# Four engine programs of a fused transformer kernel, up to the main loop, written out in another order

## The reference

```python
x = x + tanh(g_xattn[0]) * L0_xattn(layernorm(x), ctx)   # softmax(query key^T) of the context mixes x
x = x + tanh(g_ffn[0])   * L0_ffn(layernorm(x))          # 8-bit activations, ternary weights, 704 wide
x = x + tanh(g_xattn[1]) * L1_xattn(layernorm(x), ctx)   # 16 heads of 128, rmsnorm on q and k, Wo
x = x + tanh(g_ffn[1])   * L1_ffn(layernorm(x))          # 64 experts, top 8, and a shared expert

def bit_linear(x, w, g):      # used twice in L0_ffn, with silu(gate) * up between
    xn = rms_norm(x, g)
    scale = 127 / clip(max|xn|, 1e-5);  xq = clip(round(xn * scale), -128, 127) / scale
    return xq @ weight_quant(w).T
```

## Time and profile before

| | |
|---|---|
| median of 3 runs | 615.78 us (615.51 to 616.06) |
| the profiled execution, its own time | 616.09 us |
| its span | 614.3 us |
| TensorE busy | 603.3 us (98%) |
| VectorE busy | 477.9 us (78%) |
| ScalarE busy | 422.7 us (69%) |
| GpSimd busy | 236.7 us (39%) |
| granted TensorE clock | 1.00 of full speed, all through |

### The profile page before, as it was taken

One profiled execution on the slowest core, in us unless ns is written; L12 is line 12 of the kernel. 1 busy time (PEld: TensorE's weight loads), 2 busy tenths in 40 slices (PEclk: granted clock), 3 DMA queues, 4 the chain that ended last, 5 costly groups with the idle time before them and its releaser, 6 DMA issues.

```text
span 614.3 us, 11619 instructions
## 1 busy us (share of the span) xinstructions
PE 603.3 (98%) x3644; PEld 522.6 (85%) x3644; DVE 477.9 (78%) x1139; ACT 422.7 (69%) x1082; POOL 236.7 (39%) x282
## 2 busy tenths in 40 slices
PE   8979999999999999999999999999999999999997
PEld 6757899999999999999998888888887888887886
DVE  3999988987777787688876787788777676777776
ACT  6999999888888888889897344465444444443442
POOL 5999998576665566656662020000000000000000
PEclk9999999999999999999999999999999999999999
DMA  8513202000000000000030545453856466545640
GB/s 299 196 53 102 95 11 78 2 2 2 2 2 2 1 2 2 1 2 1 11 121 3 170 147 154 129 171 96 216 156 167 116 176 175 156 154 149 195 128 34
DMA packets 33653, 56.47 MB, mean 92 GB/s; under 512 B 12800, under 2 KB 13504, under 8 KB 33600
## 3 DMA queue, kind: packets, MB, share of 16 engines
q1 hardware_dynamic: 33312, 55.82, 30.4%
q10 hardware_dynamic: 288, 0.00, 0.0%
HBM read 53.45 MB, written 1.31 MB: 89 GB/s over the span
## 4 chain that ended last, share of the span: by engine, by line
PE 89%; DVE 5%; ACT 4%; issue 1%; POOL 1%; DVEq 0%; ACTq 0%; POOLq 0%
PE bank L310 25%; PE bank L312 25%; PE bank L311 25%; PE bank L985 4%; PE bank L960 2%; PE bank L952 2%; DVE hs L2088 1%; PE bank L912 1%; PE bank L1026 1%; PE bank L829 1%; DVE attT_lo L2182 1%; PE bank L835 1%; ACT att L1575 1%; ACT w L1478 1%; PE bank L815 1%
## 5 line engine op out<-in xcount | busy, mean ns | idle before, releaser
L1623 ACT ACTIVATE inter_hi<-inter 128x512 fp32r<-128x512 f32 x63 | 39.8, 632 | 140.5 <-DVE inter L2287 140.5
L310 PE MATMUL bank<-xnT_hi,front_hi 128*128 128x512 f32 (+1 forms) x260 | 102.0, 392 | 0.0
L312 PE MATMUL bank<-xnT_hi,front_lo 128*128 128x512 f32 (+1 forms) x260 | 101.7, 391 | 0.0
L311 PE MATMUL bank<-xnT_lo,front_hi 128*128 128x512 f32 (+1 forms) x260 | 101.6, 391 | 0.0
L2291 DVE TENSOR_TENSOR inter_lo<-inter,inter_hi 128x512 fp32r<-128x512 f32 x63 | 43.6, 692 | 37.9 <-ACT inter_hi L1623 37.3
L1575 ACT ACTIVATE att<-bank,shift,rq 128x256 f32<-128x256 f32 x128 | 71.3, 572 | 0.0
L596 POOL TENSOR_TENSOR att<-att,rowinv 128x512 f32<-128x512 f32 x60 | 63.1, 1067 | 11.1 <-DVE rowinv L2187 11.1
L2260 DVE TENSOR_TENSOR prod<-gate_s,bank 128x512 f32<-128x512 f32 x63 | 43.3, 687 | 21.6 <-PE bank L312 19.5
L2170 DVE TENSOR_REDUCE rowmax<-bank 128x2 f32<-128x512 f32 x64 | 43.6, 686 | 20.7 <-PE bank L312 20.4
L311 PEld LDWEIGHTS bank<-xnT_lo,front_hi 128*128 128x128 f32 x260 | 48.9, 188 | 11.3
L312 PEld LDWEIGHTS bank<-xnT_hi,front_lo 128*128 128x128 f32 x260 | 48.8, 188 | 11.3
(11 more groups left out here) (273 smaller groups left out, 1811.7 us busy)
## 6 DMA issues: line engine op xcount, KB each, us to landing
w_all<-w_rows SPq DMA_DIRECT2D x128, 128.0 KB, 3.0
raw<-in_expert_w SPq DMA_DIRECT2D x32, 384.0 KB, 3.5
wvo_raw<-in_expert_w SPq DMA_DIRECT2D x16, 384.0 KB, 3.5
e_more<-in_expert_w SPq DMA_DIRECT2D x16, 384.0 KB, 3.6
raw<-in_head_qk SPq DMA_DIRECT2D x8, 384.0 KB, 3.1
wvo_raw<-in_head_vo SPq DMA_DIRECT2D x4, 384.0 KB, 3.8
w_keep<-in_head_vo SPq DMA_DIRECT2D x4, 384.0 KB, 3.3
gate_raw<-in_gate_wT SPq DMA_DIRECT2D x2, 704.0 KB, 9.0
```

The source lines that it names most:

```text
L310: pe.matmul(out, l_hi, r_hi_, start=start, stop=False, skip_group_check=True)
L311: pe.matmul(out, l_hi, r_lo_, start=False, stop=False, skip_group_check=True)
L312: return pe.matmul(out, l_lo, r_hi_, start=False, stop=stop, skip_group_check=True)
L1623: act.activation(inter_hi[:, slot, :], inter[:, slot, :], ACT.Copy).then_inc(a_Ihi, 1)
```

## The change

No call is added or removed, but for waits: the calls of the four lists stand in another order, and TensorE's list has more `wait_ge` lines, most of them for values that a later wait of the same place implies. GpSimd gets a wait for `v_Klo` ahead of `root_3(1)`, and ScalarE one for `v_tg` ahead of `high_m(1, 7)`. SyncE's transfers, the loop and all that follows are as before.

```diff
TensorE
+            turn_att(2, 4)
             sum_abs([0, 1], 0)
-            turn_att(2, 4)
+            turn_rows_0(2, 7)
+            pe.wait_ge(t_abs, 1)
             pe.wait_ge(v_abs, 1)
             mix(1, 0)
-            sum_abs([2], 5)
-            turn_rows_0(2, 7)
-            fuse_vo(0, 6)
+            mix(2, 4)
+            pe.wait_ge(t_oA, 2)
             pe.wait_ge(v_xA, 2)
             keep_busy(0, 8)
             turn_q1(0, 0)
-            pe.wait_ge(a_x0, 3)
-            turn_q1(1, 7)
+            sum_abs([2], 5)
+            fuse_vo(0, 6)
+            pe.wait_ge(t_abs, 2)
+            pe.wait_ge(v_abs, 3)
+            proj_k(0, 5, True)
             gate_0(0)
             up_0(0)
-            mix(2, 4)
+            turn_q1(1, 7)
             gate_0(1)
...
+            gate_0(6)
+            pe.wait_ge(t_y2, 1)
+            pe.wait_ge(v_xB, 1)
+            fuse_vo(3, 6)
             turn_q1(7, 5)
-            gate_0(6)
-            pe.wait_ge(v_xB, 2)
+            pe.wait_ge(t_M, 3)
+            pe.wait_ge(a_Mhi, 3)
+            turn_q2(2, 4)
             up_0(6)
-            fuse_vo(3, 6)
             gate_0(7)
+            down(2, 5)
             up_0(7)
-            turn_q2(2, 4)
ScalarE
             abs_down()
-            split_w(0)
             turn_gate(0)
-            exp_A(3, 3)
-            copy_att(2, 4)
+            load_table(ACT.Silu)
             turn_gate(1)
-            copy_rows_0(2, 7)
             copy_q1(0, 0)
-            load_table(ACT.Silu)
+            high_ctx()
             silu_0(0)
VectorE
+            max_A(0, 2)
             stats_0(0)
             aggr_0(0)
             stats_0(1)
-            max_A(0, 2)
             max_A(1, 6)
...
             absmax_2(4)
-            round_2(2)
-            times_up_0(6)
             low_m(1, 7)
-            round_2(3)
-            absmax_2(5)
-            low_w(2)
             times_up_0(7)
             low_rows(0, 0, 1)
+            low_k(0, 0)
+            absmax_2(5)
GpSimd
             round_gate(1)
             power_1(0)
             root_1(1)
+            scale_back_1(0)
+            power_0(3)
+            scale_gain(g2, l_g2)
+            normalise_0(6)
+            limit_1(0)
+            normalise_0(7)
             power_1(1)
```

More of the change, by code:

```diff
@@ L1128, in _ @@
             gate_0(4)
-            fuse_vo(1, 7)
+            proj_k(1, 6, True)
+            up_0(4)
+            pe.wait_ge(t_y1, 5)
             pe.wait_ge(a_s1, 5)
@@ L1175, in _ @@
             turn_k(1, 0)
+            turn_q2(4, 2)
+            pe.wait_ge(t_y2, 4)
+            pe.wait_ge(v_xB, 4)
+            turn_q(1, 3)
             turn_q2(5, 6)
-            pe.wait_ge(a_q2, 5)
-            down(4, 2)
-            turn_q(1, 3)
             pe.wait_ge(a_sqQ, 8)
             proj_k(3, 4, True)
+            down(4, 2)
+            pe.wait_ge(t_q2, 6)
             pe.wait_ge(a_q2, 6)
             turn_q2(6, 6)
-            fuse_vo(6, 5)
+            scores(0)
+            pe.wait_ge(t_K, 4)
@@ L1196, in _ @@
+            scores(1)
+            proj_k(4, 3, True)
             proj_q(3, 4, True)
-            down(7, 7)
-            pe.wait_ge(v_Qlo, 2)
-            proj_k(4, 3, True)
-            pe.wait_ge(a_exp, 4)
-            scores(1)
+            pe.wait_ge(a_sqQ, 12)
+            turn(0, 0)
+            pe.wait_ge(t_K, 5)
+            pe.wait_ge(a_rawK, 5)
+            turn(0, 1)
+            pe.wait_ge(v_Klo, 3)
+            fuse_vo(7, 6)
+            proj_q(4, 5, True)
             pe.wait_ge(v_xB, 8)
@@ L1263, in _ @@
             output(2, 1)
[L1264 removed]
+            turn(4, 0)
             values(3)
[L1266 removed]
             scores(5)
[L1268 removed]
+            pe.wait_ge(v_Qlo, 7)
+            proj_q(8, 7, True)
             pe.wait_ge(a_sqQ, 32)
@@ L1722, in _ @@
             copy_q2(1, 4)
-            square_h(4)
+            act.wait_ge(v_tg, 8)
             high_m(1, 7)
             copy_q1(6, 5)
+            square_h(4)
+            split_w(2)
+            whole_m(2, 4)
             square_h(5)
-            whole_m(2, 4)
+            silu_0(6)
             copy_q1(7, 5)
-            silu_0(6)
-            split_w(2)
+            copy_q2(2, 4)
             split_w(3)
@@ L2338, in _ @@
             round_1(0)
-            inv_A(3)
+            norm_A(3)
             round_1(1)
-            norm_A(3)
+            weight_scale(1, 5, INTER * HID)
+            add_A(2, 4)
             absmax_1(1)
-            low_w(0)
+            stats_1(2)
+            inv_scale(1)
             inv_max_1(1)
+            aggr_1(2)
             round_down()
             scales_1(1)
+            times_g1(4)
             times_up_0(0)
+            times_g1(5)
             round_1(2)
-            add_A(2, 4)
+            low_m(0, 6)
+            times_up_0(1)
             round_1(3)
-            stats_1(2)
-            times_up_0(1)
-            aggr_1(2)
-            times_g1(4)
-            times_g1(5)
-            key_gain()
             absmax_1(2)
@@ L2492, in _ @@
             row_shift(4)
-            split_m(4)
-            mean_q(5)
+            low_q(5, 3)
+            low_rows(3, 3, 7)
+            low_o(2)
+            split_m(5)
             row_inverse(4, 0)
```

532 lines of the change are left out of this document (271 added, 261 removed).

## The result

The changed kernel takes **618.09 us** (median of 5 runs, 618.08 to 619.58) beside 615.74 us for the kernel before (615.23 to 616.06): 1.0048 times as long, 95% interval 1.0037 to 1.0059. By the medians it is slower by 2.35 us (the ratio takes in all runs), where the forecast was 614.5 us with a range of 612.7 to 616.9. Its runs stand at two levels, 618.1 and 619.5 us; the profiled execution is one of the upper, with 619.53 us and a span of 617.7. A second profile of the same kernel, further down, is one of the lower.

A forecast was written before the change was run, and what follows sets the result against it. TensorE's idle time in the front, before the loop's first matmul, sets the time, with VectorE, ScalarE and GpSimd full before 54 us. Terms -1.1 + 0.3 - 0.3 - 0.2 = -1.3 us gave 614.5 us, range 612.7 to 616.9.

The forecast's parts named there:

- An unknown cost: VectorE and GpSimd instructions drawn out side by side on the path: bounds 0 and +1.6 us, taken as 0.
- The first gate matmuls: TensorE at gate_0(0): about 1.4 us late but with 2.5 us more work done, -1.1 us.
- The first product: times_up_0(0) at 30.0 us, 1.6 us late behind power_1(1); VectorE has done 1.6 us of other work by then.
- The last gate and up: Around 52 to 57 us: smaller lead at up_0(7), +0.3 us; earlier times_up_0(7) and proj_q(0), -0.3 us.
- To the loop: From proj_q(0) to 126 us: waits met in time, and the 0.20 us wait for o_lo goes away, -0.2 us.
- The late power decides: Rival: power_1(1) ends after 30 us and delays the first product and what follows; sum +1.3, 617.1 us; chance 0.15.
- A stall near 80 us: Rival: split_m(2) and split_m(3) ahead of add_down(7) make TensorE wait before turn_q(2); some 616.5 us; chance 0.08.
- The lead is lost again: Rival: the three full engines lose the 1 us lead by 56 us; no change, about 615.5 us; chance 0.27.

The follow-up runs named there:

- experiment 1: The changed kernel with VectorE's round_1(2) moved up by one call, ahead of times_g1(5): 616.48 us, ratio 1.0013 to the kernel before.
- experiment 4: The changed kernel measured again, word for word: 618.02 us, ratio 1.0041 to the kernel before, all runs at the lower level.
- experiment 2: The changed kernel with GpSimd's power_1(1) back directly behind root_1(1): 618.17 us, ratio 1.0038 to the kernel before.
- experiment 12: Experiment 1's kernel with VectorE's low_q(1) moved ahead of add_down(5) only, and a TensorE wait ahead of proj_q(3): 616.30 us, ratio 1.0015 to the kernel before.
- experiment 10: Experiment 1's kernel with VectorE's low_w(2) five calls later, behind low_k(0): 619.87 us, ratio 1.0072 to the kernel before.

## Why the prediction was wrong

**What failed** is the step "An unknown cost", in these words: "My lengths are the short ones. [...] I take 0". The lengths of the old timeline were carried over to an order in which other pairs of instructions lie side by side. The meeting that came was not the one examined (`power_1(1)` with `round_down`: the power took 1.10 us where it had 0.89) but `round_1(2)` with `times_gain(0)`: 1.4 us of wait, by experiment 1 worth 1.5 us of the time, and about 1.1 us more where the clock falls. The wait lay inside the bound of +1.6 us; what was wrong was to take one end of it for the likeliest, and to have no term for the clock. Without this meeting the kernel is still 0.8 us slower than before, so the step explains 1.5 of the 3.6 us between forecast and result; the rest is in the terms below.

**The first gate matmuls, -1.1 us:** right in kind, a little smaller. By 28 us TensorE has done 0.91 us more than before, `mix(2)` and `proj_k(0)` ahead of `gate_0(0)`. That this one came at 27.32 us (27.4 to 27.6 forecast) is partly luck: 0.63 us of it is the lag of that execution. In the other profile it is at 26.69 us, 0.5 us behind before where 1.4 were forecast.

**The first product:** `times_up_0(0)` at 29.86 us (30.0 forecast), again with the lag; without it 29.23 us, 0.8 us late and not 1.6. TensorE loses 0.85 us between 28 and 31 us, nearly all of the lead, and the prediction's sum had no term for that: 0.25 us are `up_0(1)` waiting for this product, and 0.60 us are `gate_0(1)` waiting for `copy_q1(1)`, which stands behind `silu_0(0)` and was covered by `mix(2)` before. VectorE's other work gives back what was forecast for the products: `times_up_0(2)`, at 37.60 us before, is at 37.13 us in the changed kernel at full clock (0.6 us ahead forecast), and at 35.72 in experiment 1, where 1.3 to 1.9 us of lead last up to the sixth product. The seventh is ahead by 0.1 us only (51.34 against 51.45); what takes this lead was not tested by itself.

**The last gate and up, +0.3 and -0.3 us:** wrong by about 0.8 us (0.80 us more idle time between 33.5 and 60 us at full clock, where the two terms add up to 0). `times_up_0(7)` doesn't only wait for VectorE's queue; it waits 0.85 us for `times_gain(5)` to leave the buffer of h, and that stands behind both `normalise_1` and a `power_3(0)` that takes 1.80 us beside `round_2(3)` and `low_w(2)`. GpSimd's list was counted for its work, not for the buffer it frees.

**To the loop, -0.2 us and no wait over 0.1 us:** the wait at 113.91 us did go. But 0.8 us came between 60 and 100 us, 0.48 of it at `scores(1)`, which the new list puts ahead of two projections that had covered `low_q(1)`.

**The sum.** In place of -1.1 + 0 + 0.3 - 0.3 - 0.2 = -1.3 us the traces of full clock show, stretch by stretch, -0.90 + 0.85 + 0.59 + 0.80 + 0.81 - 0.20 = +1.95 us of idle time from 10 us on (the changed kernel of experiment 4 against the kernel before). The two profiled executions are 1.9 us apart (616.2 and 614.3 us of span, 617.97 and 616.09 us of time), so these terms account for them. The medians are 2.35 and 2.5 us apart because the profiled execution of before lies 0.35 to 0.6 us above the medians of its runs, 615.74 and 615.51.

**The rivals.** "The late power decides" had the right sign and about the right time, 617.1 us, for the wrong reason: experiment 2 takes the late power away and gets nothing. "A stall near 80 us" named the wrong call; `split_m` stopped nobody. "The lead is lost again" (615.5 us) is nearest to what experiment 1 shows, though that is at 616.5 us.

## What to carry to other kernels

Where two engines are both full and can hold each other up, the length of an instruction is not a property of the instruction but of the order: list which calls of each read and write SBUF alone (reductions kept their lengths here), lay the new order of both side by side, and price each call that would start while the other engine is within one of these at the rest of that one's length. Take a second profile of the same kernel before reading differences under 1 us off the first. Before moving a call of one engine, follow what it frees as well as what it makes, the load queue included. And measure a whole set of lists together: one list out of a fitted set cost 24 us, and of the five local repairs on top of the swap four only moved the wait or made a new meeting, while the fifth (experiment 12) gained nothing that could be measured.

## What had not been expected of the hardware

- An instruction on two to four numbers a partition took 2.31 us (`scales_1(2)`, its like 0.18) and 1.71 us (`mean_k`'s last, 0.17 in the changed kernel) beside a GpSimd tensor_tensor of 2.36 and 1.85 us.
- GpSimd is held up the same way: `power_3(0)` takes 1.80 us with `low_w(2)` beside it, 0.93 us without (experiment 10), and 0.71 us in the kernel before.
- The same wait of 1.40 us was followed by a clock of 0.50 in one profile and of 1.00 in the other, of one and the same kernel. The runs of the two kinds lie 1.4 us apart; in the two profiles, 0.63 us of the difference was there before the wait.
